# Recurrent part of a two-layer block: fp32r gates, four up banks, the feeding half first

## What is computed

```
xn = layernorm(x)
s  = network(xn)              # a recurrent network, below
g  = silu(xn W' + low-rank update + bias)      # the gate, 512x512
x  = x + s * g

network(v):
  h = v Win + bin                         # 512 -> 64 features
  4 times (l):
    y = silu(layernorm(h) * l1w + l1b)
    y = real part of a complex recurrence along the 1024 tokens (one pole per feature)
    h = h + y * scl
    y = silu(layernorm(h, l2w, l2b) W1 + b1)     # 64 -> 256
    h = h + y W2 + b2                            # 256 -> 64
  return layernorm(h, lnl_w, lnl_b) Wout + bout  # 64 -> 512
```

## Time and profile before

| | us |
|---|---|
| median of 3 runs (645.24 to 645.54) | 645.26 |
| the profiled execution | 645.43 |
| its span, first to last instruction | 643.6 |
| PE busy | 610.8 |
| DVE busy | 481.3 |
| ACT busy | 329.6 |
| POOL busy | 183.9 |

### The profile page before, as it was taken

How to read it: one execution, slowest core, us unless ns; L and a number is a source line. 1 busy time by engine, 2 the same in 40 slices (tenths; PEclk the granted TensorE clock), 3 DMA queues, 4 the chain that set the end, 5 groups by cost and what they waited for, 6 DMA issues and landing times. The chain is left out here.

```text
span 643.6 us, 8635 instructions
## 1 busy us (share of the span) xinstructions
PE 610.8 (95%) x2788; PEld 448.5 (70%) x2788; DVE 481.3 (75%) x912; ACT 329.6 (51%) x551; POOL 183.9 (29%) x303
## 2 busy tenths in 40 slices
PE   8969999999999999999999999999799999999875
PEld 6857887888888888888888888877544444444332
DVE  6998799897888788789788778776576555555456
ACT  6758477267438428617735752846434334343320
POOL 2432002001001000200200100498865555543234
PEclk9979999999999999999999999999899999999887
DMA  8801000110020030020020001450300000000015
GB/s 345 316 13 67 0 2 1 66 34 2 20 78 0 0 98 0 0 98 0 0 64 33 0 1 66 162 209 2 68 1 0 1 0 0 2 1 1 0 65 197
DMA packets 17197, 32.34 MB, mean 50 GB/s; under 512 B 3240, under 2 KB 3752, under 8 KB 17168
## 3 DMA queue, kind: packets, MB, share of 16 engines
q1 hardware_dynamic: 17168, 31.99, 14.3%
HBM read 24.63 MB, written 7.35 MB: 50 GB/s over the span
## 5 line engine op out<-in xcount | busy, mean ns | idle before, releaser
L849 DVE TENSOR_SCALAR_CACHE_REDUCE junk_d<-k_buf,cand 128x1376 int8<-128x1376 f32 x56 | 91.8, 1640 | 0.3
L645 ACT ACTIVATE junk_a<-k_buf,cand 128x1376 int8<-128x1376 f32 x56 | 80.5, 1437 | 0.6
L1181 PE MATMUL ps_a<-wd_hi,zt_hi 128*128 128x512 f32 (+1 forms) x176 | 71.9, 409 | 0.2 <-DVE zt_lo L968 0.2
L624 ACT ACTIVATE s_buf<-ps_a 128x1376 f32<-128x1376 f32 x16 | 21.1, 1319 | 94.0 <-PE ps_a L1148 89.4
L1181 PE MATMUL ps_a<-wd_hi,zt_lo 128*128 128x512 f32 (+1 forms) x176 | 69.2, 393 | 0.0
L1181 PE MATMUL ps_a<-wd_lo,zt_hi 128*128 128x512 f32 (+1 forms) x176 | 68.9, 391 | 0.0
L1901 PE MATMUL ps_b<-arena,xt 128*128 128x512 f32 x128 | 63.6, 611 | 0.0
L522 POOL TENSOR_TENSOR xres<-xres,gate 128x512 f32<-128x512 f32 x12 | 22.3, 1860 | 130.9 <-DVE gate L975 130.9
L1148 PE MATMUL ps_b<-wu_hi,xt_hi 128*128 128x512 f32 (+1 forms) x192 | 52.4, 381 | 0.0
L514 POOL TENSOR_TENSOR rstd<-var_eps,expo 128x2 f32<-128x2 f32 x7 | 4.9, 703 | 164.9 <-DVE var_eps L771 164.9
L1148 PE MATMUL ps_a<-wg_hi,xt_hi 128*128 128x512 f32 (+1 forms) x192 | 51.9, 378 | 0.0
(11 more groups left out here) (235 smaller groups left out, 1314.5 us busy)
## 6 DMA issues: line engine op xcount, KB each, us to landing
xres<-in_x SPq DMA_DIRECT2D x8, 512.0 KB, 3.3
out<-arena SPq DMA_DIRECT2D x16, 256.0 KB, 2.1
xin<-in_x SPq DMA_DIRECT2D x7, 512.0 KB, 4.1
x_scratch<-xres SPq DMA_DIRECT2D x6, 514.0 KB, 4.0
arena<-x_scratch SPq DMA_DIRECT2D x3, 1028.0 KB, 12.8
m_buf<-in_wg_t SPq DMA_DIRECT2D x2, 688.0 KB, 5.0
k_buf<-in_wg_t SPq DMA_DIRECT2D x2, 688.0 KB, 7.9
m_buf<-in_wu_t SPq DMA_DIRECT2D x2, 688.0 KB, 7.5
```

Of the source, the lines that this page charges most:

```text
L624: act.activation(s_buf[:, t, :], ps_a[:].rearrange("p a n -> p (a n)")[:, 0:INNER], ACT.Silu).then_inc(s_ready, 1)
L645: act.activation(junk_a[:], k_buf[:, 1, :], ACT.Sign, bias=c, scale=-1.0, accum_out=below[:, 1:2]).then_inc(act_step, 1)
L849: dve.tensor_scalar(junk_d[:], k_buf[:, 0, :], c, -float(DROP), ALU.is_lt, ALU.add, accum_out=e).then_inc(cnt_dve, 1)
L1181: last = pe.matmul(ps_a[:, t, :], zs, ws[0:rows, c, :], start=(c == 0 and n == 0), stop=(c == CHUNKS - 1 and n == 2))
```

## The change

Block A's end: `weff` becomes two fp32r tensors, high and low part. ScalarE rounds (4 instructions), VectorE subtracts (4, `weights_low`), between the last two `down_gate`.

Block B: token tiles are split the same way (`split_hi` on ScalarE, `split_lo` on VectorE, 128x512 each, a ring of four). A gate product is three fp32r products, high-high, high-low, low-high: 13 steps a tile instead of 5, dealt out by new counts. The bias row's product takes 128 rows instead of 64. The up products use four banks and are issued together. The recurrence's scale goes into `turn_back`; its real part is added to h by itself (`add_real`), the imaginary part by `into_h`. The feeding half's norm comes ahead of the mixing half's on all engines. `hand_over` (the carry to the other half) moves behind `fed`. On GpSimd the table products move behind both roots and between the two `times_sin`, and the first `times_sin` waits for VectorE's turn. `g2` shares its memory with `xt`, which is laid out by tile.

```
-GATE_STEPS = 2 * (KH + 1)
-GATES = (1, 2, 1, 3, 2, 1)
+SPLIT = 4
+PRODUCTS = 3 * KH
+GATES = (3, 5, 5, 1, 2, 10)
...
# block A, scalar: at the end
+                for k in range(KH):
+                    act.wait_ge(free, k + 1)
+                    act.activation(weff_hi[:, k, :], f_wt[:, k, :], ACT.Copy).then_inc(weff_h, 1)
# block A, vector
-                    dve.tensor_tensor(weff[:, k, :], bankf[k % 2], f_wt[:, k, :], ALU.add).then_inc(free, 1)
+                    dve.tensor_tensor(f_wt[:, k, :], bankf[k % 2], f_wt[:, k, :], ALU.add).then_inc(free, 1)
+
+                def weights_low(k):
+                    dve.wait_ge(weff_h, k + 1)
+                    dve.tensor_tensor(weff_lo[:, k, :], f_wt[:, k, :], weff_hi[:, k, :].bitcast(F32),
+                                      ALU.subtract).then_inc(weff_l, 1)
...
                     down_gate(p + 1, 0)
+                    for k in range(KH):
+                        weights_low(k)
                     down_gate(p + 1, 1)
# block B
-            xt = sb("xt", [P, KH, TOKENS])
-            g2 = sb("g2", [P, TILES, HID])
+            xt = sb("xt", [P, TILES, HID])
+            g2 = xt
+            xs_hi = sb("xs_hi", [P, SPLIT, KH, P], F32R)
+            xs_lo = sb("xs_lo", [P, SPLIT, KH, P], F32R)
...
+            def up_bank(c, u):
+                return (bankx + [bank1[1 - c], bank2[c]])[u]
# gpsimd
                     pool.wait_ge(ready[c], count)
+                    if src is y:
+                        pool.wait_ge(cv_wr[c], l + 1)
...
-                    if l < DEPTH:
-                        if phase == 1:
-                            pool.wait_ge(h_ready[0], 2)
-                        else:
-                            pool.wait_ge(h_ready[c], 2 * l + 1)
-                        tables_some(5 + 3 * phase, 7 + 3 * phase)
-                    root(2 * l, c)
                     if feeds:
                         root(2 * k + 1, d)
+                    root(2 * l, c)
                     if l < DEPTH:
-                        pool.wait_ge(ln_w[d], 2 * k + 2)
-                        tables_some(7 + 3 * phase, 8 + 3 * phase)
-                    if l < DEPTH:
+                        tables_some(5 + 3 * phase, 7 + 3 * phase)
                         pool.wait_ge(tb, N_SMALL + 6 * l + 6)
                         times_sin(l, c, y, ln_o, 2 * l + 1, cv_wi)
+                        tables_some(7 + 3 * phase, 8 + 3 * phase)
                         times_sin(l, c, u_im, cv_ui, l + 1, cv_b)
# scalar, phase loop
+                    if feeds:
+                        squares(n, d)
                     squares(q, c)
                     if feeds:
-                        squares(n, d)
                         centered(n, d)
-                    if phase == 1:
-                        gate(1)
+                    if phase < PHASES - 1:
+                        gate(2 * phase - 1)
+                    if feeds:
+                        norm_out(n, d, ACT.Identity, pcol(k, C_L2W), pcol(k, C_L2B))
                     if l < DEPTH:
+                        gate(2 * phase)
                         norm_out(q, c, ACT.Silu, pcol(l, C_L1W), pcol(l, C_L1B))
...
                         for u in range(4):
                             hidden(k, d, u)
-                            if u == 2 and l < DEPTH:
-                                gate(2 * phase + 1)
+                    if splits:
+                        for j in range(2, 4):
+                            split_hi(2 * phase + j)
# vector
 def turn_back(l, c):
-                    dve.tensor_tensor(w_re[:, cs(c)], u_re[:, cs(c)], rot_c[:, l, :], ALU.mult).then_inc(cv_a[c], 1)
+                    dve.scalar_tensor_tensor(out=w_re[:, cs(c)], in0=u_re[:, cs(c)], scalar=pcol(l, C_SCL),
+                                             in1=rot_c[:, l, :], op0=ALU.mult, op1=ALU.mult).then_inc(cv_a[c], 1)
+
+                def add_real(l, c):
+                    dve.wait_ge(cv_a[c], l + 1)
+                    dve.tensor_tensor(h[:, cs(c)], h[:, cs(c)], w_re[:, cs(c)], ALU.add).then_inc(cv_ab[c], 1)
...
 def into_h(l, c):
-                    dve.wait_ge(cv_a[c], l + 1)
+                    dve.wait_ge(cv_ab[c], l + 1)
                     dve.wait_ge(cv_b[c], l + 1)
-                    dve.tensor_tensor(w_re[:, cs(c)], w_re[:, cs(c)], w_im[:, cs(c)], ALU.add).then_inc(cv_ab[c], 1)
-                    dve.wait_ge(cv_ab[c], l + 1)
-                    dve.scalar_tensor_tensor(out=h[:, cs(c)], in0=w_re[:, cs(c)], scalar=pcol(l, C_SCL),
+                    dve.scalar_tensor_tensor(out=h[:, cs(c)], in0=w_im[:, cs(c)], scalar=pcol(l, C_SCL),
                                              in1=h[:, cs(c)], op0=ALU.mult, op1=ALU.add).then_inc(h_ready[c], 1)
...
+                def split_lo(k):
+                    t = ORDERED[k]
+                    dve.wait_ge(xs_h, k + 1)
+                    dve.tensor_tensor(xs_lo[:, k % SPLIT, :, :], xt[:, t, :].rearrange("p (k n) -> p k n", k=KH),
+                                      xs_hi[:, k % SPLIT, :, :].bitcast(F32), ALU.subtract).then_inc(xs_l, 1)
...
                     if phase:
-                        variance(q, c)
                         if feeds:
                             variance(n, d)
+                        if l < DEPTH:
+                            split_lo(2 * phase)
+                        variance(q, c)
+                        if l < DEPTH:
+                            split_lo(2 * phase + 1)
...
-                        widen(q, c)
-                        normed(q, c)
                         if feeds:
                             widen(n, d)
                             normed(n, d)
+                        widen(q, c)
+                        normed(q, c)
                     if l < DEPTH:
                         turn(l, c)
                         scan(l, c, False)
                         scan(l, c, True)
                         turn_back(l, c)
-                        if c == 0:
-                            hand_over(l)
+                        add_real(l, c)
                         into_h(l, c)
                         if feeds:
                             fed(k, d)
+                        if c == 0:
+                            hand_over(l)
...
# tensor, gate_step
+                    j = n % KH
+                    xs, ws = ((xs_hi, weff_hi), (xs_hi, weff_lo), (xs_lo, weff_hi))[n // KH]
+                    pe.matmul(bankg[k % 2], xs[:, k % SPLIT, j, :], ws[:, j, :], start=(n == 0), stop=False)
# tensor, phase loop of the changed kernel
                     if feeds:
                         center_rows(n, d)
+                        gates(fill[0])
                         variances(n, d)
+                        variances(q, c)
+                        gates(fill[1])
                         spread(n, d)
+                        gates(fill[2])
+                        spread(q, c)
                         gates(fill[3])
...
+                        for u in range(4):
                             up_unit(k, d, u)
                         gates(fill[4])
                         if l == DEPTH:
...
                             output(0)
                             output(1)
+                        for u in range(4):
+                            down_unit(k, d, u)
                         gates(fill[5])
                         if l == DEPTH:
                             output(2)
                             output(3)
```

More of the change, by code:

```diff
@@ L1780, in _ @@
                 dve.tensor_copy(bias_c[:], bank2[0][:, 0:DEPTH + 1]).then_inc(bc_s, 1)
+                for k in range(2):
+                    split_lo(k)
                 dve.wait_ge(bc_s, 1)
@@ L1837, in _ @@
                         h_in(1)
-                        take_means(w2[:], KH, 2 * DEPTH, w2_s)
             @block_b.tensor
```

113 lines of the change are left out of this document (58 added, 55 removed).

## The result

| us | before | after |
|---|---|---|
| median (lowest to highest) | 645.4 (645.24 to 647.01, 4 runs) | 667.46 (666.2 to 668.59, 4 runs) |
| profiled execution, span | 645.43, 643.6 | 666.2, 664.4 |
| first centering (end of all that lies ahead of phase 1) | 482.85 | 486.73 |
| phases 1 to 7, centering to centering | 16.91, 17.34, 17.33, 17.34, 17.34, 16.91, 16.92 | 19.82, 19.50, 20.62, 20.53, 20.49, 19.70, 17.36 |
| of each at TensorE's lower clock | none | 6.8, 3.6, 7.0, 6.9, 6.8, 6.4, 0 |

The change makes the kernel slower: ratio 1.0336 (95% interval 1.0316 to 1.0356). The forecast was 656.8, between 644 and 665: the direction is right, the size is not, and the median lies 2.5 us outside the range. Of the 20.8 us between the two profiled executions 3.9 lie ahead of phase 1, 17.9 in the seven phases, and the end gives back 1.0.

What follows compares the result with a forecast made beforehand. TensorE looked like the bound before, the mixing chain after. 645.43 + 2.4 (first part's end) + 1.0 (before phase 1) + 10.2 (phases 1 to 7) - 2.2 (end) = 656.8 us; range for 8 in 10: 644 to 665.

Steps and rivals of the forecast that it cites:

- rival 2: Recurrent phases: TensorE's clock falls inside them, lengthening the chain some 1.2 us a phase, 665 us; chance 14 in 100.
- Who takes over: Recurrent phases: TensorE's work falls by more than the mixing chain's 1.5 us of slack, so that chain becomes the bound.
- Gates: TensorE's gate products, 7 us a phase, become 24 taking 5.4 us; its work falls to about 14.3 to 14.9 us.
- The chain, feeding first: Mixing chain behind the feeding half: next centering at +17.35 us for 16.92, +0.43 us a phase without tables.
- Tables: Phases 1 to 5: moved GpSimd table products delay second widen by 0.87 us and imaginary scan by 0.80; phases take 19.0.
- The end of the first part: Block A's end: four weights_low each take about 0.6 us from GpSimd's table chain, +2.4 us.
- Before phase 1: Start of the second part: split_lo, take_means and y times sine meet GpSimd's tables and VectorE's work, together +1.0 us.
- The end: From phase 8 on: feeding first saves 2 to 4.5 us, later outputs give back about 1.2; net -2.2 us.
- Rival 3: GpSimd roots keep the shared port, so each second split_lo waits and pushes the first widen; 660.3 us; chance 10 in 100.
- Rival 1: VectorE and GpSimd collisions don't happen, phases take 16.97 us, first part ends as before; 640 us; chance 20 in 100.

Runs made afterwards that it cites:

- e2: The changed kernel with the GpSimd table products back where they were before the change; 652.38 us, ratio 1.0106.
- e5: The changed kernel with mixing half first, table products in their old places and y times sine not waiting for turn; 648.81 us, ratio 1.0038.
- e8: The changed kernel with both 14 unread filler products a phase on TensorE and the old table places; 653.87 us, ratio 1.0109.
- e10: The changed kernel with both split_lo of a phase moved from between variance and root; 665.1 us, ratio 1.0295.
- e4: The changed kernel with the mixing half first again in every step from squares to spreads; 655.16 us, ratio 1.015.
- e1: The changed kernel with 14 unread filler products a phase on TensorE in phases 1 to 7; 662.5 us, ratio 1.0271.
- e9: Against e6: weights_low moved into the second part, work before phase 1 reordered, four input tiles kept off the gate weights; 636.67 us, ratio 0.984.
- e6: Against e5: gate steps dealt out anew, two split_lo moved, first two table products released by the previous into_h; 642.2 us, ratio 0.9929.

## Why the prediction was right in direction and wrong in size

- **The step that failed** is rival 2, "TensorE's clock falls inside the phases": it got 14 in 100 and nothing in the sum. Without it a table phase is 19.05 us, phase 6 18.28 and phase 7 17.36, 130.9 us in all. Measured were 138.0. **7.1 us** are the clock's; the sum's error in the profiled execution is 9.4. The other 2.3 are 0.5 ahead of phase 1, 0.6 in the phases and 1.2 at the end. Of the 0.6, 0.4 is a reading: I took phase 1 of before at 17.33 us, and it was 16.91.
- *The time that I gave for this rival*, 665, is what the profiled execution took within 1.2 us (the median is 2.5 above it). That is luck in part: its 8 us are near the 7.1, but the falls came in six phases, each at another price than the even 1.2, and the 2.3 us of the other terms aren't in it.
- *What I argued against it* was that a gate run stands on either side of each gap. That didn't hold. There are two kinds of falls in after. Four stand right at a centering (the ends of phases 2 to 5), where PE had idled 2.5 us. Here the gate run behind the centering (three products, 2.25 us in phase 3) ran at half clock with it. Six stand around the first spread (phases 1 to 6), where gate products had run just ahead and PE had been busy 2.8 to 3.4 of the 3.4 us before. The other argument, that the fall of before resembled the new phases, was the right one. That fall comes at 606.40, 3.5 us behind the centering of phase 8, and not at the end of phase 7's work: PE had then been busy 2.97 of 3.42 us with a centering and variances. It is of the second kind.
- *The length of the gap* orders only the first kind. Behind 2.5 us the clock fell, behind the 1.73 us of phase 7 it didn't. But phase 2, whose centering stands behind 1.60 us, has a fall around its first spread, and so have phase 4 of e2, behind the same 1.74 us as its neighbours, and phases of e5 and e8 with no gap ahead of the centering.
- *Its price* was mis-sized too. I took the same 1.2 us for each phase; measured are 0.45 us in phase 2, 0.8 in phase 1 and 1.4 to 1.6 in phases 3 to 6. In phases 3 to 6 the first widen stands at +6.36 to +6.46 for +5.20, so 1.2 us of it is the slow centering and the gate run behind it, and the fall at the spread adds little, because the late widen misses part of its meeting with the table product. Where no product is in its way (e2, e5, e8) one fall at the spread costs 1.2 to 1.4 us (0.9 in phase 1 of e2). The page of the Trainium skill "TensorE: Matmul & The Clock Gate", section Terms, puts the penalty at the throttled time by the share of clock lost. Here this would be half of 37.5, an estimate of 18.8 us; the phases show 7.1, because most of that time fell in work nobody waited for. The measurement decides.
- **Who takes over** was right: the mixing chain bounds each phase, and the feeding half is never late.
- **Gates** were right: PE's work in phase 7 fell from 16.66 to 14.96 us, just above the 14.3 to 14.9 worked out.
- **The chain, feeding first**, was right to 0.01 us in phase 7, and three runs show its terms by the end of into_h or the phase: 0.38 for split_lo (e10), 1.39 for the order (e4, +15.91 for +17.30) and 0.67 for the product behind turn (e5, +15.24). Of the last two only 0.92 reached the phase (16.44 for 17.36), where TensorE took over.
- **Tables** were right. At full clock widen takes 1.33 (forecast 1.3) and the imaginary scan 2.08 (forecast 1.28 + 0.80). A table phase has 19.05 for 19.0, and the tables' part, forecast as 1.67, is 1.69 over phase 7, of which putting them back gives 1.47 (e2) or 1.44 (e8). In after itself the second widen took 0.86, since the spread ahead of it was late.
- **The end of the first part**: the second part began 2.6 us later, as forecast 2.4, but by luck. The memset at 445.15 in after, ahead of weights_low, is already 1.0 us late against 444.14 before, which is scatter; from there weights_low adds 1.6, not 2.4: 0.4 for each of the four, not 0.6.
- **Before phase 1** +1.25 for +1.0.
- **The end** gave 1.0, not 2.2. The addition came at +16.71, inside my bounds of +14.1 to +17, at the late end, since the clock was low from 628.22 to 638.46.
- **Rival 3** fell. The second split_lo at 611.28 took its usual 0.68 us inside a root that had begun before it, and so did that of each of the seven phases. By the rule of the Trainium skill, "SBUF — State Buffer", section Who interferes with whom, it would wait; where a root of 128x8 has begun, the trace does not agree. Beside products of 128x512 it does: in e1 the widen ended 0.28 us behind the product, and the scan 1.08.
- **Rival 1** fell too: all meetings happened.

That the clock's falls make the phases longer is shown by e1, where a table phase without a fall takes 19.29 us, fillers included; the 7.1 us are worked out from it. What stays open is what brings each single fall. Idle time alone doesn't: in e8 a phase without any fell, and its neighbours, with the same work, didn't. All falls around a spread come behind a centering and two-column products, but so do the phases without one, and the mean clock of one kernel differs between executions (e5, e9).

## What to carry to other kernels

Taking a tenth of its work from an engine that bounds a loop hands the loop to the next chain; if that engine is TensorE, look at the granted clock in each phase too, and not only at the chain. The gain was there, but the work stood in the wrong order: mixing first (e4), the tables back in their places (e5), and then the gate steps, two splits and the table products' release moved (e6), made a slower kernel a faster one. A meeting of two engines costs what the loop's slack doesn't cover, and more if the clock falls with it: 2.9 us in one kernel, 15.1 in the other, for the same products. Before a difference of a microsecond or two is put down to an edit, compare a mark ahead of it: here the unchanged first part alone moved by 2 us. Put GpSimd's spare products where VectorE waits for someone else.

## What the runs showed of the hardware that was not expected

- In after TensorE's granted clock went to 0.50 right at four centerings, each behind an idle gap of 2.5 us, and stayed at 1.00 behind the gap of 1.73 us ahead of phase 7. It also fell around the first spread of six phases, where PE had been busy 2.8 to 3.4 of the 3.4 us before. In each case it came back while PE worked on.
- The same work doesn't always have the same clock: phase 4 of e2 and phase 6 of e8 have a fall that their neighbours don't have, and a fall of 3.4 us costs anything from 0.35 (e1) to 1.43 us (e2), by what waits for the slowed spread.
- Filler products that nobody reads kept most phases at full clock, but cost 0.2 to 0.5 us a phase themselves. In e1 phases 1 to 7 took 133.9 us for 138.0, in e8 126.3 for 124.9.
- A VectorE subtraction with two SBUF inputs took its usual 0.68 us inside a GpSimd root that had begun 0.7 us before (seven times in after), while the root behind such a subtraction took 2.01 us for 1.62.
- Two executions of one kernel differ by up to 6.5 us (e5, 645.5 at a mean clock of 0.971, 652.0 at 0.959). Where the clock was low in the second wasn't seen.
